# Layer 1 on one Trainium2 core: chosen rows moved by rank with indirect DMAs instead of products with a selection matrix, and GpSimd's products in pairs

## The chip, the core and the metric

The kernel runs on one core of a Trainium2 chip. A core has a matrix engine (PE in the profile, its weight loads PEld), a vector engine (DVE), a scalar engine (ACT), a general engine (POOL, GpSimd) and a queue engine that issues most transfers (SP). Each runs its own instruction list in order; they meet through semaphores, and sixteen DMA engines move data between the device's memory and SBUF. The time is the device time of the whole program in microseconds; lower is better.

## The reference, cut to what matters

The input is (8, 512, 256) in float32. Layer 0 (gated linear attention and a mixture of experts) is untouched by the change. Layer 1 adds two branches to its input: a selective state-space scan, and a mix of light local attention over windows of 128 rows and heavy attention of 256 chosen rows of each batch element against all 512:

```
xn = _layernorm(x)
x  = x + L1_attn(xn) + L1_ffn(xn)

# L1_attn: state-space scan, 512 channels x 16 states, over 512 steps
h = exp(delta[..., None] * A) * h + delta[..., None] * B[:, None, :] * u[..., None]
y = einsum('bds,bs->bd', h, C)
out = einsum('btm,dm->btd', (y + D*u) * silu(z), W_out)

# L1_ffn
light_out = light_local_attn(x, ...)
scores_q, idx_q = route(x, q_routing_token, NQ)      # NQ = 256 of the 512 rows
routed_q = take_along_axis(x, idx_q)
routed_out = heavy_attn(routed_q, x, ...)
heavy_out = zeros_like(x).at[arange(b)[:, None], idx_q].set(routed_out)
return light_out + heavy_out
```

Each row's *rank* by its score decides whether it is chosen (rank under 256) and in which place it stands among the chosen.

## The kernel before, in words

Layer 0 takes the first 770 us or so; then layer 1 runs one batch element after the other, with the stages of neighbouring elements overlapping. Every engine's list in layer 1 is written from one table, `AT` (`FIRST` and `LAST` for the first and last element): it gives each step of an element a number, the steps of all elements (number plus `PERIOD` times the element) are sorted, and every engine issues its own steps in that sorted order. The numbers set an order only. PSUM banks 3 to 7 are dealt out in the same order (`Banks`); banks 0 to 2 belong to the scan.

**The scan.** The 512x16 states are cut into 64 chunks of 128 partitions by 512 steps. For chunk n, POOL writes the drive (`dbu`, `drive`, L2042) into slot n mod 8 of the ring `HB`; ACT writes the decay (`dA`) into a PSUM bank; DVE scans (`scan`, L2596). The product with C is DVE's for even chunks (`mult`, L2601) and POOL's for odd ones (`cg`, `times_c`, L2048). PE sums four chunks at a time over the states (`fold`), which frees four slots of the ring: a drive waits for the fold of two groups before. Then come `skip` (DVE), `gate` (POOL, L2052), and `tail` (PE), the output product. POOL also does `del` and `du` (L2068, L2075) for the next element.

**The attention.** Projections, scores, maxima, exponentials, transposes (`turn`), values, normalisation and the output product (`widen`) run for four light tiles and two heavy ones. The light results are added to `X` by DVE (`widenc`), the heavy ones go to `YR` (`widenr`, ACT).

**The chosen rows.** DVE counts the rank of each row (`rank`, `ranks`: L2579 to L2590). POOL turns the ranks into a 0/1 matrix `Sel` of 4x128 rows by 256 places (`sel`, L2062). PE multiplies the rows with it (`xg`, `gather`: eight products of 128x256), which gives the chosen rows already transposed. PE also transposes `Sel` (`st`, L2172, eight transposes), ACT copies it to `SelT` (`sta`, `stv`), and in `tail` two products with `SelT` per tile of 128 rows add the heavy outputs back at their rows in the same PSUM bank. `tailc` (DVE) adds the bank to `X`, `out` stores it, and `x_ld` loads the next element's `X` once all four tiles are stored. Float32 products run as two instructions each in the trace, so eight products appear as x16; transposes appear once.

Layer 0 already has indirect DMAs of this kind: POOL scatters rows of 1 KB to device memory by a slot number (`sca`, L581) and gathers them back while adding (`gad`, L591).

## Time and profile before

| | us |
|---|---|
| median of 3 runs | 1994.58 (1978.45 to 1995.64) |
| the profiled execution, its own time | 2009.35 |
| its span | 2007.2 |
| PE busy | 1817.3 (91%) |
| DVE busy | 1566.5 (78%) |
| POOL busy | 1504.5 (75%) |
| ACT busy | 1345.0 (67%) |

The shares are averages over two layers with different limits. From about 930 us to 1820 us the trace of layer 1 repeats with a period of 148.5 us; that stretch is where an average of one period can be read. Matmuls are pipelined and their ends are modelled, so a busy PE is not PE at its peak.

### The profile page before, as it was taken

How to read it: one execution, taken by the hardware profiler on the slowest of the kernel's cores; microseconds unless marked ns; L12 is line 12 of the kernel's file. 1: busy time of each engine (PE TensorE's matmuls, PEld its weight loads, DVE VectorE, ACT ScalarE, POOL GpSimd, SP SyncE). 2: the span in 40 equal slices, each digit the busy share in tenths (PEclk: the TensorE clock that was granted, in tenths of full speed). 3: DMA queues.
4: the chain of work that ended last, by engine and by line, in shares of the span. 5: the costliest groups of instructions: out<-in, count | busy, mean ns of one | idle time of the engine just before them, and what ended most of it. 6: DMA issues, size and time to landing. Idle time of an engine off the chain costs nothing.

```text
span 2007.2 us, 44199 instructions
## 1 busy us (share of the span) xinstructions
PE 1817.3 (91%) x13543; PEld 1159.6 (58%) x13543; DVE 1566.5 (78%) x2833; ACT 1345.0 (67%) x3152; POOL 1504.5 (75%) x1211
## 2 busy tenths in 40 slices
PE   6889989989999947897999999999999999998897
PEld 4577777767777724543644644644644644644554
DVE  5766756666666543899899889999999989988896
ACT  3465456337546426687788788788888788787674
POOL 2834663593557431789989989989989989988996
PEclk9888889679888878898999999999999999999899
DMA  8234244344525575333642732642633644542530
GB/s 276 86 99 125 73 115 138 73 111 112 127 61 140 131 179 166 97 101 112 178 127 90 179 113 90 174 117 98 172 112 109 160 118 120 144 133 96 143 84 22
DMA packets 162135, 245.76 MB, mean 122 GB/s; under 512 B 32712, under 2 KB 107112, under 8 KB 161904
## 3 DMA queue, kind: packets, MB, share of 16 engines
q1 hardware_dynamic: 149616, 226.15, 39.7%
q0 software_dynamic: 12288, 16.79, 4.2%
q8 instruction: 113, 1.85, 0.4%
q14 instruction: 118, 0.97, 0.2%
HBM read 169.39 MB, written 73.47 MB: 121 GB/s over the span
## 4 chain that ended last, share of the span: by engine, by line
PE 28%; POOL 13%; issue 8%; DVE 6%; DMA 4%; ACT 2%; SPq 2%; POOLq 0%; DVEq 0%; ACTq 0%
PE bank L2097 24%; POOL HB L2042 8%; POOL HB L2048 4%; PE bank L2200 2%; DVE bank L2596 2%; SPq L1973 2%; DVE HB L2596 1%; DMA BC<-ssm_scratch 1%; DMA X<-x_scratch 1%; POOL SD L2068 1%; DMA out<-X 1%; PE bank L2106 1%; DMA dd_scratch<-U 1%; POOL U L2075 1%; PE bank L2228 1%
## 5 line engine op out<-in xcount | busy, mean ns | idle before, releaser
L2042 POOL TENSOR_TENSOR HB<-DD,BC 128x512 f32<-128x512 f32 x512 | 642.8, 1281 | 81.0 <-PE bank L2097 60.4
L2388 ACT ACTIVATE bank<-DD,A 128x512 f32<-128x512 f32 x512 | 351.9, 691 | 114.7 <-DVE HB L2601 61.5
L2048 POOL TENSOR_TENSOR HB<-HB,BC 128x512 f32<-128x512 f32 x256 | 324.5, 1281 | 20.3 <-DVE HB L2596 20.3
L2596 DVE TENSOR_TENSOR_SCAN bank<-bank,HB 128x512 f32<-128x512 f32 x256 | 311.4, 1216 | 32.8 <-ACT bank L2388 18.9
L2596 DVE TENSOR_TENSOR_SCAN HB<-bank,HB 128x512 f32<-128x512 f32 x256 | 310.4, 1212 | 19.9 <-POOL HB L2042 15.8
L2601 DVE TENSOR_TENSOR HB<-bank,BC 128x512 f32<-128x512 f32 x256 | 175.7, 686 | 15.3 <-DVE bank L2596 0.5
L2097 PE MATMUL bank<-HB,fold 128*32 128x512 f32 x1024 | 140.9, 622 | 33.8 <-POOL HB L2048 17.7
L591 POOL DMA_INDIRECT X<-expert_out_scratch,slot x64 | 101.2, 1580 | 54.5 <-DMA expert_out_scratch<-YS 39.1
L2200 PEld LDWEIGHTS bank<-ident,PR 128*128 128x128 f32 x768 | 89.3, 144 | 76.3 <-issue 44.1
L2097 PE MATMUL bank<-Ka,Qa 64*128 64x128 f32 (+1 forms) x768 | 112.9, 413 | 16.0 <-ACT PT L2322 14.2
L2200 PE MATMUL bank<-ident,PR 128*128 128x128 f32 x768 | 115.8, 283 | 12.3 <-ACT PR L2426 10.3
L557 POOL TENSOR_TENSOR ROW<-ROW,COL 128x1024 f32<-128x1024 f32 x32 | 66.6, 2082 | 80.0 <-DMA ROW<-row_scratch 67.4
L2097 PE MATMUL bank<-Wv,XRT 128*128 128x512 f32 x256 | 124.8, 621 | 0.1
L2097 PE MATMUL bank<-XRT,Wk 128*128 128x512 f32 x256 | 123.0, 606 | 1.1 <-ACT Qa L2402 0.7
L2097 PE MATMUL bank<-XT,edge 128*128 128x512 f32 x256 | 121.0, 611 | 3.3 <-ACT SD L2322 2.2
L2322 ACT ACTIVATE PT<-bank 128x512 f32<-128x512 f32 x192 | 109.4, 591 | 8.2 <-PE bank L2200 6.6
L2097 PEld LDWEIGHTS bank<-PT,Va 128*64 128x64 f32 x1536 | 83.0, 137 | 47.6 <-issue 37.0
L620 PE MATMUL bank<-v,AT 64*64 64x16 f32 x2048 | 93.8, 237 | 16.1 <-DVE S L1230 6.9
L571 POOL TENSOR_SCALAR XSC<-edge,weight 128x256 f32<-128x256 f32 x64 | 62.0, 977 | 57.0 <-DVE weight L1178 55.8
L620 PEld LDWEIGHTS bank<-v,AT 64*64 64x64 f32 x2048 | 89.2, 180 | 25.6 <-issue 20.8
L2097 PE MATMUL bank<-PT,Va 128*64 128x128 f32 x1536 | 102.4, 279 | 0.1
L2426 ACT ACTIVATE PR<-bank,nmax 128x512 f32<-128x512 f32 x128 | 87.0, 682 | 20.2 <-DVE nmax L2620 20.1
(280 smaller groups left out, 4218.4 us busy)
## 6 DMA issues: line engine op xcount, KB each, us to landing
DD<-dd_scratch SPq DMA_DIRECT2D x512, 128.0 KB, 3.6
ROW<-row_scratch SPq DMA_DIRECT2D x64, 256.0 KB
BC<-ssm_scratch SPq DMA_DIRECT2D x128, 128.0 KB, 4.9
US<-us_scratch SPq DMA_DIRECT2D x32, 512.0 KB, 5.5
XL<-sorted_scratch SPq DMA_DIRECT2D x92, 128.0 KB, 2.7
expert_out_scratch<-YS SPq DMA_DIRECT2D x92, 128.0 KB, 1.9
us_scratch<-U SPq DMA_DIRECT2D x8, 1024.0 KB, 4.2
us_scratch<-SD SPq DMA_DIRECT2D x8, 1024.0 KB, 6.5
```

The source lines that it names most:

```text
L557: done(pool.tensor_tensor(ROW[:, t % 2], ROW[:, t % 2], bc(COL[:, t], CH), ALU.subtract), "df")
L591: pool.indirect_dma_start(X[:, b % 2, t], None, scr["expert_out"][g % 2], bass.IndirectOffsetOnAxis(slot[:, g % 2, x, c:c + 1], 0), comput ...
L620: return pe.matmul(out, lhsT, rhs, start=start, stop=stop)
L2042: done(pool.tensor_tensor(HB[:, c % HR], du, bc, ALU.mult), "dbu")
L2048: done(pool.tensor_tensor(h, h, bc, ALU.mult), "cg")
L2097: return pe.matmul(out, lhsT, rhs, start=start, stop=stop)
L2200: q = pe.transpose(bank[:, j * P:(j + 1) * P], PR[:, m % 2, j * P:(j + 1) * P], ident[:])
L2322: done(act.activation(dst, banks.of[made, b, i][:], ACT.Copy), copy)
L2388: done(act.activation(PD[n % 2][:], delta, ACT.Exp, scale=A[:, k:k + 1]), "dA")
L2426: done(act.activation(PR[:, m % 2], banks.of["score", b, m][:], ACT.Exp, bias=nmax[:, m % 4, 0:1], accum_out=sums[:, a, h:h + 1]), "exp")
L2596: done(dve.tensor_tensor_scan(h if n % 2 else dA, dA, h, 0.0, ALU.mult, ALU.add), "scan")
L2601: done(dve.tensor_tensor(HB[:, (NCH * b + n) % HR], PD[n % 2][:], bc, ALU.mult), "mult")
```

## The change

1. **Pairs on POOL.** `dbu` now writes two chunks with one instruction of 128x1024 (32 per element instead of 64), and `cg` multiplies two odd chunks at once (slots c and c+2; 16 instead of 32). A scan waits for the pair, a `cg` for both of its scans.
2. **Choosing.** `Sel`, `SelT`, `sel`, `st`, `sta`, `stv` are gone. DVE copies the ranks to integers (`slot`). POOL scatters the four tiles of rows by rank to device memory (`scat`, four indirect DMAs), SP loads the first 256 places as `XQ` (`ql`), and PE transposes them (four transposes instead of eight products).
3. **Adding.** SP stores `YR` to device memory (`ys`), whose places 256 to 511 were zeroed once at the start, and POOL gathers all 512 rows by rank and adds them to `X` (`gad`, four indirect DMAs). `tail` is left with the products of the scan; `tailc` waits for the gather of its tile.
4. The table of numbers is another one.

Its core:

```diff
-PERIOD = 177.597
+PERIOD = 212.24
 AT = {
...
+    "slot": [-12.224],
+    "scat": [-6.013, -11.242, -0.19, -11.573],
+    "gad": [236.605, 243.002, 261.958, 243.453],
+    "ql": [26.232],
+    "ys": [234.633],
...
                 def h_load(b):
-                    after(sp, "xg", b - 1, 0)
+                    after(sp, "xrt", b - 1, *range(ND))
+                    sp.wait_ge(moved["rows_out"], 16 * NT * b)
...
+                def chosen_load(b):
+                    sp.wait_ge(moved["rows_out"], 16 * NT * (b + 1))
+                    after(sp, "xg", b - 1, 0)
+                    sp.dma_start(XQ[:], scr["ranked"][b % 2][0:NQ].rearrange("(j p) d -> p j d", p=P)).then_inc(over["q_in"], 16)
+
+                def chosen_store(b):
...
+                    after(sp, "widenr", b, *range(NQT))
...
+                    sp.dma_start(scr["heavy_out"][b % 2][0:NQ].rearrange("(j p) d -> p j d", p=P), YR[:]).then_inc(over["y_out"], 16)
...
-                def drive(b, n):
+                def drive(b, i):
...
-                    done(pool.tensor_tensor(HB[:, c % HR], du, bc, ALU.mult), "dbu")
+                    du = DD[:, g % DDS:g % DDS + 2, 1]
+                    done(pool.tensor_tensor(HB[:, c % HR:c % HR + 2], du, bc.unsqueeze(1).broadcast_to([P, 2, T]), ALU.mult), "dbu")
...
-                    after(pool, "scan", b, n)
-                    done(pool.tensor_tensor(h, h, bc, ALU.mult), "cg")
+                    h = HB[:, c:c + 3:2]
+                    after(pool, "scan", b, n, n + 2)
+                    done(pool.tensor_tensor(h, h, bc.unsqueeze(1).broadcast_to([P, 2, T]), ALU.mult), "cg")
...
-                def select(b, t):
...
-                    done(pool.tensor_scalar(Sel[:, t], numbers[:], ties[:, t:t + 1], None, ALU.is_equal), "sel")
+                def rank_rows(b, t):
+                    after(pool, "slot", b, 0)
+                    after(pool, "xr", b, t)
...
+                    pool.indirect_dma_start(scr["ranked"][b % 2], bass.IndirectOffsetOnAxis(slot[:, b % 2, t:t + 1], 0),
+                                            XN[:, t], None).then_inc(moved["rows_out"], 16)
+
+                def add_heavy_rows(b, t):
+                    after(pool, "widenc", b, t)
+                    pool.wait_ge(over["y_zero"], 32)
+                    pool.wait_ge(over["y_out"], 16 * (b + 1))
+                    pool.indirect_dma_start(X[:, t], None, scr["heavy_out"][b % 2],
+                                            bass.IndirectOffsetOnAxis(slot[:, b % 2, t:t + 1], 0),
+                                            compute_op=ALU.add).then_inc(moved[f"heavy_add{t}"], 16)
...
-                        for t in range(NT):
-                            q = mm(bank[:, k * NQ:(k + 1) * NQ], XN[:, t, k * P:(k + 1) * P], Sel[:, t],
-                                   t == 0, t == NT - 1)
+                        for j in range(NQT):
+                            q = pe.transpose(bank[:, k * NQ + j * P:k * NQ + (j + 1) * P], XQ[:, j, k * P:(k + 1) * P], ident[:])
...
-                    for j in range(NQT):
-                        q = mm(bank[:, 0:D], SelT[:, j, t * P:(t + 1) * P], YR[:, j], False, j == NQT - 1)
...
+                def slots(b):
+                    after(dve, "ranks", b, 0)
...
+                    done(dve.tensor_copy(slot[:, b % 2], ties[:]), "slot")
...
                 def tail(b, t):
                     after(dve, "tail", b, t)
-                    after(dve, "widenc", b, t)
+                    dve.wait_ge(moved[f"heavy_add{t}"], 16 * (b + 1))
```

The order of instructions at three places. In these rows HB<-DD,BC is a drive, HB<-HB,BC a product with C, "Wout,G" the tail's products of the scan, "YR,SelT" those of the heavy outputs.

First, POOL where one element ends and the next begins. Before:

```order
L2042 TENSOR_TENSOR HB<-DD,BC 128x512
L2048 TENSOR_TENSOR HB<-HB,BC 128x512 x2
L2062 TENSOR_SCALAR Sel<-numbers,ties 128x256
L2048 TENSOR_TENSOR HB<-HB,BC 128x512 x2
L2042 TENSOR_TENSOR HB<-DD,BC 128x512 x5
L2048 TENSOR_TENSOR HB<-HB,BC 128x512 x2
L2042 TENSOR_TENSOR HB<-DD,BC 128x512
L2052 TENSOR_TENSOR G<-G,US 128x512
L2042 TENSOR_TENSOR HB<-DD,BC 128x512 x4
L2048 TENSOR_TENSOR HB<-HB,BC 128x512 x2
L2042 TENSOR_TENSOR HB<-DD,BC 128x512 x2
L2062 TENSOR_SCALAR Sel<-numbers,ties 128x256
```

After:

```order
L2079 DMA ranked_scratch<-edge,slot 512x256
L2056 TENSOR_TENSOR HB<-DD,BC 128x1024 x2
L2064 TENSOR_TENSOR HB<-HB,BC 128x2x512
L2056 TENSOR_TENSOR HB<-DD,BC 128x1024
L2068 TENSOR_TENSOR G<-G,US 128x512
L2056 TENSOR_TENSOR HB<-DD,BC 128x1024 x2
L2086 DMA X<-heavy_out_scratch,slot 128x256
L2064 TENSOR_TENSOR HB<-HB,BC 128x2x512
L2086 DMA X<-heavy_out_scratch,slot 128x256 x2
L2056 TENSOR_TENSOR HB<-DD,BC 128x1024 x2
L2064 TENSOR_TENSOR HB<-HB,BC 128x2x512
L2086 DMA X<-heavy_out_scratch,slot 128x256
```

Each drive or product in the second list covers two chunks. Three more scatters stand just ahead of the second list; the gathers that add stand among the first drives of the next element, as one, two and one.

Second, PE at the tails and the choice of rows. Before:

```order
L2097 MATMUL bank<-Wout,G 128x256 x4
L2097 MATMUL bank<-YR,SelT 128x256 x2
L2097 MATMUL bank<-HB,fold 32x512 x4
L2200 MATMUL bank<-ident,PR 128x128 x4
L2097 MATMUL bank<-Wout,G 128x256 x4
L2097 MATMUL bank<-YR,SelT 128x256 x2
L2228 MATMUL bank<-ident,RX 128x128 x4
L2200 MATMUL bank<-ident,PR 128x128 x4
L2097 MATMUL bank<-Ka,Qa 128x128 x8
L2172 MATMUL bank<-ident,Sel 128x128 x4
L2097 MATMUL bank<-Sel,edge 128x256 x8
L2097 MATMUL bank<-HB,fold 32x512 x4
```

After:

```order
L2219 MATMUL bank<-ident,PR 128x128 x8
L2125 MATMUL bank<-Ka,Qa 128x128 x8
L2125 MATMUL bank<-Wout,G 128x256 x4
L2125 MATMUL bank<-HB,fold 32x512 x4
L2191 MATMUL bank<-ident,XQ 128x128 x4
L2125 MATMUL bank<-Wout,G 128x256 x8
L2125 MATMUL bank<-PT,Va 64x128 x8
L2219 MATMUL bank<-ident,PR 128x128 x4
L2148 MATMUL bank<-ident,edge 128x128 x4
L2219 MATMUL bank<-ident,PR 128x128 x4
```

The products with SelT and Sel and the transposes of Sel are gone, and four transposes of XQ stand between the tails.

Third, the end of POOL's list. Before:

```order
L2042 TENSOR_TENSOR HB<-DD,BC 128x512 x4
L2048 TENSOR_TENSOR HB<-HB,BC 128x512
L2042 TENSOR_TENSOR HB<-DD,BC 128x512
L2048 TENSOR_TENSOR HB<-HB,BC 128x512 x3
L2052 TENSOR_TENSOR G<-G,US 128x512
```

After:

```order
L2056 TENSOR_TENSOR HB<-DD,BC 128x1024 x2
L2064 TENSOR_TENSOR HB<-HB,BC 128x2x512
L2056 TENSOR_TENSOR HB<-DD,BC 128x1024
L2064 TENSOR_TENSOR HB<-HB,BC 128x2x512
L2086 DMA X<-heavy_out_scratch,slot 128x256
L2068 TENSOR_TENSOR G<-G,US 128x512
L2086 DMA X<-heavy_out_scratch,slot 128x256 x3
```

A gather now stands ahead of the last gate, and three behind it.

## Rows read from the trace of the kernel before

**Rows 1.** Busy time by engine in two periods of layer 1: PE, PEld, DVE, ACT, POOL (instructions).
```profile
1229.50:1378.00 148.50, 142.05 (x812) 79.25 (x808) 134.54 (x182) 122.26 (x265) 137.76 (x110) 1.00 0.46 129
1378.00:1526.50 148.50, 142.44 (x814) 79.26 (x811) 137.22 (x182) 123.42 (x266) 138.21 (x110) 1.00 0.46 129
```

**Rows 2.** Chain that ended last: start, us, what; over one period of layer 1.
```profile
1230.07 2.34 POOL SD L2068
...
1274.46 9.03 PE bank L2097 x44
...
1323.58 19.41 PE bank L2097 x80
...
1378.61 2.34 POOL SD L2068
```

**Rows 3.** PE groups by shape, 1274 to 1304 us alone: busy, mean ns | idle before, releaser.
```profile
L2097 PE MATMUL bank<-YR,SelT 128*128 128x256 f32 x16 | 4.1, 379 | 0.0
...
L2097 PE MATMUL bank<-Sel,edge 128*128 128x256 f32 x16 | 3.6, 379 | 0.0
...
L2172 PE MATMUL bank<-ident,Sel 128*128 128x128 f32 x8 | 1.3, 279 | 0.0
```

**Rows 4.** POOL groups by shape, one period, 1229.5 to 1378 us.
```profile
L2042 POOL TENSOR_TENSOR HB<-DD,BC 128x512 f32<-128x512 f32 x65 | 81.6, 1279 | 9.6 <-PE bank L2097 7.4 <-DMA DD<-dd_scratch 2.2
...
L2048 POOL TENSOR_TENSOR HB<-HB,BC 128x512 f32<-128x512 f32 x32 | 40.5, 1280 | 0.9 <-DVE HB L2596 0.9
...
L2062 POOL TENSOR_SCALAR Sel<-numbers,ties 128x256 f32<-128x256 f32 x4 | 3.7, 929 | 0.0
...
L2075 POOL TENSOR_TENSOR U<-SD,U 128x1024 f32<-128x1024 f32 x2 | 4.7, 2360 | 0.2
```

**Rows 5.** POOL groups by shape, whole span: layer 0's indirect DMAs and a 1024-wide operation.
```profile
L591 POOL DMA_INDIRECT X<-expert_out_scratch,slot x64 | 101.2, 1580 | 54.5 <-DMA expert_out_scratch<-YS 39.1 <-issue 13.3 <-DMA X<-expert_out_scratch,slot 0.9
...
L581 POOL DMA_INDIRECT sorted_scratch<-XSC,slot x64 | 67.0, 1046 | 14.6 <-issue 8.6 <-POOL XSC L571 5.7 <-DVE edge L1054 0.3
...
L557 POOL TENSOR_TENSOR ROW<-ROW,COL 128x1024 f32<-128x1024 f32 x32 | 66.6, 2082 | 80.0 <-DMA ROW<-row_scratch 67.4 <-DVE COL L1082 12.4
```

**Rows 6.** L561 on POOL: duration ns min/median/max, first and last start.
```profile
L561 POOL TENSOR_TENSOR ROW<-ROW,later x32: 2333/2400/2947, 38.6 to 650.5; 128x1024 f32<-128x1024 f32 x32
```

**Rows 7.** DMA issues of the whole span: KB each, median us to landing.
```profile
out<-X SPq DMA_DIRECT2D x32, 128.0 KB, 1.9
...
X<-expert_out_scratch,slot POOLq DMA_INDIRECT x64, 3.9
```

**Rows 8.** DVE in the ranking: durations ns min/median/max, then L2583 as a group.
```profile
L2583 DVE SCALAR_TENSOR_TENSOR Sel<-KR,KC,before x32: 346/528/5334, 837.9 to 1854.9; 128x128 f32<-128x128 f32 x32
...
L2590 DVE TENSOR_TENSOR ties<-ties,ahead x8: 164/1146/1151, 842.5 to 1857.9; 128x4 f32<-128x4 f32 x8
...
L2583 DVE SCALAR_TENSOR_TENSOR Sel<-KR,KC,before 128x128 f32<-128x128 f32 x32 | 29.4, 920 | 0.0
```

**Rows 9.** Timeline around 1242 us, DVE then POOL: start, duration.
```profile
1241.34 1.10 DVE L2583 SCALAR_TENSOR_TENSOR Sel<-KR,KC,before 128x128 f32<-128x128 f32 x1
...
1239.78 2.51 POOL L2048 TENSOR_TENSOR HB<-HB,BC 128x512 f32<-128x512 f32 x2
```

**Rows 10.** Waits, 1229.5 to 1378 us: us in total, times, longest.
```profile
DVE bank L2596 <- POOL HB L2042: 3.0, 3, 2.0
...
DVE HB L2596 <- POOL HB L2042: 2.1, 4, 1.1
```

**Rows 11.** Timeline of the end, POOL then PE.
```profile
1992.48 1.27 POOL L2052 TENSOR_TENSOR G<-G,US 128x512 f32<-128x512 f32 x1 [2.51 <-DVE G L2609]
...
1991.52 1.99 PE L2097 MATMUL bank<-Wao,OT 128*128 128x256 f32 x8
...
1994.03 1.97 PE L2097 MATMUL bank<-Wout,G 128*128 128x256 f32 x8 [0.52 <-POOL G L2052]
...
2003.61 1.03 PE L2097 MATMUL bank<-YR,SelT 128*128 128x256 f32 x4
```

610 lines of the change are left out of this document (307 added, 303 removed), and 162 rows, old and new, of tables (AT, FIRST, LAST).

## The prediction, made before the changed kernel was timed

> **What bounds the kernel now.** I read the busy time in 10-us and 148.5-us stretches first, then the chain of waits, then the groups by shape inside one period, then the waits.
>
> Layer 0 is not touched, so everything is decided after 770 us. There the trace repeats: the same step of POOL stands in the chain at 1230.07 and at 1378.61 us [rows 2], so one batch element costs 148.5 us. In that period PE is busy for 142.0 to 142.4 us, POOL for 137.8 to 138.2, DVE for 134.5 to 137.2, ACT for about 123 [rows 1]; the clock of PE is at its full level (1.00, the 2.4 GHz one), so there is nothing to gain or lose there. Four engines are within 19 us of each other: the reader should expect that taking work from one shows up only until the next one is reached. The chain inside the period runs over PE from 1274.46 us on (stretches of 9.0 us, later 19.4 us [rows 2]) up to 1343 us, and over POOL's drives in most of the rest. I read it as: PE sets the pace for half of a period, POOL for a third.
>
> **What the change does to PE.** Removed per element: the products with SelT (4.1 us busy), the products with Sel (3.6), the transposes of Sel (1.3) [rows 3]. Added: four transposes of XQ, half of those 1.3 us, 0.65. Net -8.4 us, and all of them stand between 1274 and 1304 us [rows 3], inside the stretch where the chain is on PE. PE goes from 142.2 to 133.8 us. ACT loses two copies, about 1.2 us, and is not near the bound.
>
> **POOL.** A drive and a product with C take 1.28 us each [rows 4]; 96 of them make 122.9 us. The change makes 48 of 1024 columns. Nothing in the trace has their form exactly. Nearest is the plain 128x1024 product in the same stretch, 2.36 us [rows 4]; the one that reads an operand again and again, as the pair reads BC, has a median of 2.40 [rows 6]. The ends: 2.08 us (an operand that stands still for 64 columns [rows 5]) and 2.56 us (two singles, nothing saved). I take 2.40: 115.2 us, so -7.7 (ends -23.1 and 0). The four `sel` go: -3.7 [rows 4]. Four scatters at 1.05 and four adding gathers at 1.58 us [rows 5] come: +10.5. Before such a DMA POOL also stood idle for reasons other than the transfer it waited for: (14.6 + 54.5 - 39.1) us over 128 of them [rows 5], 0.23 each, +1.9. Sum: +1.0, so POOL goes from 138.0 to 139.0 us. POOL is not relieved at all; the pairs only pay for the DMAs. With the ends of the pair's price it is 123.6 to 146.7.
>
> **DVE.** Its removed and added work is one tiny copy (`slot`). But rows show a coupling: an operation of the ranking that reads two SBUF tensors takes 0.35 us at its shortest and 0.92 in the mean, and the tiny addition after it 1.15 instead of 0.16 [rows 8]. The one of 1.10 us ended at 1242.44, where POOL's instruction ended at 1242.29 [rows 9]: it waited for the end of what POOL was doing. Per element that is 4 x 0.57 + 1.0 = 3.3 us. When most of POOL's instructions are twice as long, a wait for the end of one is twice as long in the mean: +3.3, and `slot` may meet it too, +1. Bounds: 0 and, if every such operation met a whole pair, 6 x 2.4 = 14 less the 3.3 there now. DVE goes from 135.9 to 140.2 us. (The Trainium skill, SBUF — State Buffer, section "Who interferes with whom", has the rule behind it: GpSimd and a VectorE instruction with two SBUF inputs lock a shared port pair for the whole instruction, and the later one blocks. The trace agrees in rows 9. By a rule of shared bandwidth instead, DVE would gain no time at all and the 4.3 us would be absent from the sum.)
>
> **The new waits.** I followed each through the orders.
> - Choosing: ranks, `slot`, scatter, load, transposes. Scatters stand at the end of POOL's element, the load and the transposes after several drives of the next one. Landings of this kind take 2 to 4 us [rows 7]; covered by the drives between them (some five pairs, 12 us).
> - Adding: `ys` needs the last `widenr`, the gathers need `ys` landed, `tailc` needs the gather landed (3.9 us [rows 7]). Behind each gather stand one or two pairs or gathers on POOL before the scan that follows `tailc` on DVE can start anyway, so DVE should lose nothing. Behind a waiting gather on POOL stand the drives; the first fold of the element lies between `widen` and the gather, which covers the store.
> - `x_ld` waits for all four stores and now comes later in the element; SP has the slack (its next load of DD is needed some ten drives later). Until `widenc` the first light banks stay taken; that is the least certain cover.
> - Scans wait for a pair instead of a single drive: the first of a pair 1.1 us later, the second 0.2 earlier. A product with C waits for both scans, so the fold and the four slots of the ring come about 1.1 us later, of a turn of the ring of 18.5 us (148.5/8).
>
> **The period.** DVE is now the fullest with 140.2 us. It waited 5.1 us for POOL's drives in a period [rows 10]; POOL in turn waited 7.4 us for folds [rows 4], which come sooner on a lighter PE, while the pairs work the other way. I take 4.6 of waits: 144.8 us, -3.7 per element, -29.6 over eight.
>
> **The end.** Now the last gate runs at 1992.48, the tails start at 1994.03 and follow each other by 2.6 us [rows 11]. The tails shrink by 1 us each, three of them count: -3. The output product before them starts at 1991.52 and would come some 2 us sooner, but a gather now stands ahead of the last gate and needs the copy of that product, its store (2 to 3 us, [rows 7] with twice the size) and its own 1.58 us, so the gate comes 4 to 5 us later than without: +1.5 in all. At the start two stores of zeros go beside other work: 0.
>
> Sum -28. The profiled execution took 2009.35 us, 14.8 over the median of the three runs; the same difference applied to the median gives 1994.6 - 28 = **1966 us**, chance 0.42, its own range 1950 to 1980.
>
> **Rivals.**
> - *PE's time passes through.* If DVE's 12.6 idle us are slack and its operations slip into POOL's gaps, the period falls by PE's 8.4 us to 140.1: 1994.6 - 67 + 1.5 = 1929 us (1915 to 1950). For it: the chain hardly touches DVE. Against: POOL at 139.0 would need a share of 99%. Chance 0.19.
> - *The gain is used up.* DVE's 140.2 us keep 8.3 of their 12.6 us of waits and the period stays 148.5: about 1995 us (1975 to 2014). For it: every engine's order is new, and banks are held longer. Chance 0.20.
> - *POOL becomes the bound (slower).* If a pair costs what two singles do, 2.56 us, POOL has 146.7 us; with its waits for DD and scans (3.1) 149.8, with those for folds (7.4) 157. The middle, 153.4: +4.9 x 8 + 1.5 = 2035 us. It decides from a price of about 2.53 us a pair (139.0 - 115.2 + 48p + 3.1 = 148.5). Against it: the 1024-wide product in this very stretch takes 2.36. Chance 0.15.
> - *The DMAs on POOL wait for DVE (slower).* If writing a transfer's description waited for one scan of 1.2 us each time, eight of them make 9.8 us and POOL has 148.8, with 3.1 of waits 151.9: +3.4 x 8 + 1.5 = 2023 us. Against it: in layer 0, beside a DVE busy for 65%, a gather needed 1.58 us in the mean of 64 [rows 5]. Chance 0.04. (The Trainium skill, SBUF — State Buffer, section "SBUF: two separate sides", warns of it for VectorE's two-port modes; no row here shows it.)
>
> **The numbers.** About 1% is what a measurement of this kernel tells from no change, 20 us. Faster (under 1974.6): 0.35 of the forecast's 0.42 and the 0.19 of the first rival, 0.54. Within: 0.07 and 0.20, 0.27. Slower: 0.19. The range 1925 to 2015 leaves out the low end of the first rival (about 0.05) and the two slower ones mostly (0.15).
>
> **What the new profile would show.** PE about 134 us per period, with no SelT. Pairs on POOL of 2.36 to 2.40 us; at 2.5 and over, the POOL rival. Scatters and gathers at 1.05 and 1.6 us; longer, the last one. L2583's successor with a mean near 1.5 us. The distance of two `slot` copies is the period: 140, 145 or 148.5 tells the cases apart. If `tailc` waits for a gather, if POOL waits for the store of YR outside the last element, or if `widenc` waits over a microsecond for X, my reading of the orders was wrong. A period under 139 or over 157 would overthrow the whole account.

## The result, and the profile after

The changed kernel takes **2032.98 us** (median of 3, 2029.21 to 2035.48), against 1994.58: ratio 1.0177, 95% interval 1.0118 to 1.0236. The forecast was 1966 with a range up to 2015; it is slower, and outside the range.

The profiled execution took 2029.21 us. Layer 0 ends at another time in each execution (732 and 713 us), so I compare layer 1 alone: 1274.8 us before, 1314.9 after, +40.1. Up to the last gate of the first element it is 8.7 us more, over the six periods behind it 23.2, over the rest (one more period and the end) 8.2: the loss is in every element. The end alone, from the input of the very last gate on, got shorter, 15.5 to 14.4 us.

Busy time over three periods, before and then after (columns as in [rows 1]):

```profile
1119.13:1565.20 446.07, 426.27 (x2420) 237.60 (x2419) 406.02 (x543) 367.48 (x792) 411.97 (x327) 1.00 0.45 128
```

```profile
1117.81:1577.32 459.51, 414.62 (x2313) 221.61 (x2313) 421.43 (x547) 362.15 (x786) 413.01 (x196) 0.99 0.48 135
```

Per element PE went down by 3.9 us only (142.1 to 138.2, at a clock that is no longer full all the time), DVE up by 5.1 (135.3 to 140.5), POOL stayed (137.3 to 137.7). The period went up by 4.5. **DVE's idle time did not shrink**: (446.07 - 406.02)/3 = 13.4 us before, (459.51 - 421.43)/3 = 12.7 after. POOL's grew from 11.4 to 15.5.

The groups of POOL in that stretch, where [rows 4, 5] had the forecast's prices:

```profile
L2056 POOL TENSOR_TENSOR HB<-DD,BC 128x1024 f32<-128x1024 f32 x96 | 230.4, 2441 | 9.7 <-PE bank L2125 9.4
L2064 POOL TENSOR_TENSOR HB<-HB,BC 128x1024 f32<-128x1024 f32 x49 | 121.1, 2471 | 31.2 <-DVE HB L2605 31.2
L2086 POOL DMA_INDIRECT X<-heavy_out_scratch,slot x12 | 19.0, 1581 | 2.4 <-issue 1.9 <-DVE HB L2605 0.5
...
L2079 POOL DMA_INDIRECT ranked_scratch<-edge,slot x12 | 12.2, 1020 | 2.9 <-issue 1.7 <-DVE slot L2599 1.0 <-PE bank L2125 0.2
```

A pair lasts 2.36 us where no DMA stands before it; behind a DMA the record is some 0.6 us longer, because it begins before the DMA's record ends. So the means of 2.44 and 2.47 hold part of the DMAs. What is new is the wait of the products with C for scans: 31.2 us in three elements, 10.4 each, against 1.7 before (0.9 in the one period of [rows 4]). The waits of the drives for folds fell from 8.3 to 3.1. The sum of the two rose.

DVE in the ranking, where [rows 8] stood:

```profile
L2584 DVE SCALAR_TENSOR_TENSOR KJ<-KR,KC,before 128x128 f32<-128x128 f32 x12 | 22.4, 1863 | 0.0
L2599 DVE CAST slot<-ties 128x4 int32<-128x4 f32 x3 | 4.5, 1493 | 0.0
L2590 DVE TENSOR_TENSOR ties<-ties,ahead 128x4 f32<-128x4 f32 x3 | 3.5, 1177 | 0.0
```

And the timeline (start, duration) around the longest of them, first DVE, then POOL:

```profile
1231.40 5.86 DVE L2584 SCALAR_TENSOR_TENSOR KJ<-KR,KC,before 128x128 f32<-128x128 f32 x1
```

```profile
1230.11 4.70 POOL L2101 TENSOR_TENSOR U<-SD,U 128x1024 f32<-128x1024 f32 x2
1234.76 2.35 POOL L2056 TENSOR_TENSOR HB<-DD,BC 128x1024 f32<-128x1024 f32 x1
1240.81 2.35 POOL L2064 TENSOR_TENSOR HB<-HB,BC 128x1024 f32<-128x1024 f32 x1 [3.70 <-DVE HB L2605]
```

An operation that takes 0.34 us alone took 5.86. It did not end with the POOL instruction that ran when it started (until about 1232.5), nor with the next one (1234.8), but at 1237.26, after the third, behind which POOL first had a gap (1237.11). Then POOL stood idle for 3.70 us, waiting for a scan that stood behind this very operation in DVE's list.

A gap is not what it needs, though. Two elements later the same operation started beside the same instructions of POOL, again without a gap between them, and ended behind the first of them:

```profile
1540.93 1.23 DVE L2584 SCALAR_TENSOR_TENSOR KJ<-KR,KC,before 128x128 f32<-128x128 f32 x1
```

```profile
1539.63 4.74 POOL L2101 TENSOR_TENSOR U<-SD,U 128x1024 f32<-128x1024 f32 x2
1544.33 2.42 POOL L2056 TENSOR_TENSOR HB<-DD,BC 128x1024 f32<-128x1024 f32 x1
```

So it is let in at the end of a POOL instruction, but not at every one. No run here shows what decides it.

**Stages.** To see where a period gets longer I cut it at every eighth of its 64 scans on DVE (starts in the timeline, mean of four periods in the middle of layer 1; stage 1 begins with the first scan after the last gate's input). "Old order" and "new order" are the two tables of numbers; the kernels are told with the experiments.

| kernel | ratio to before | 1 | 2 | 3 | 4 | 5 | 6 | 7 | 8 | period |
|---|---|---|---|---|---|---|---|---|---|---|
| before | 1 | 14.3 | 16.7 | 21.1 | 20.5 | 15.5 | 20.7 | 23.4 | 16.3 | 148.4 |
| after | 1.018 | **19.3** | 16.9 | 19.7 | 18.8 | 15.5 | 19.4 | **26.3** | 17.0 | 152.9 |
| pairs, old order | 1.023 | 14.5 | 18.0 | 21.6 | 19.5 | 16.6 | 20.5 | 25.1 | 16.3 | 152.0 |
| DMAs, old order | 1.036 | **21.6** | 16.8 | 20.8 | 20.4 | 15.5 | 20.7 | 24.5 | 16.3 | 156.6 |
| both, old order | 1.050 | **21.4** | 17.7 | 21.5 | 19.4 | 16.6 | 20.5 | 25.3 | 16.4 | 158.7 |
| DMAs, new order | 1.035 | 19.0 | 18.6 | 20.5 | 18.8 | 15.4 | 21.0 | 27.9 | 17.7 | 158.9 |
| drives in pairs only | 1.014 | 14.7 | 17.0 | 20.5 | 19.8 | 17.7 | 19.4 | 26.3 | 15.7 | 151.3 |
| products in pairs only | 1.005 | 14.2 | 16.4 | 21.8 | 19.9 | 14.5 | 21.6 | 23.9 | 16.5 | 148.8 |
| less PE, stages 1 to 2 | 0.998 | 14.5 | 17.8 | 20.8 | 20.8 | 15.5 | 20.7 | 23.4 | 16.1 | 149.5 |
| less PE, stages 3 to 4 | 0.990 | 14.4 | 16.1 | 20.2 | **19.3** | 15.5 | 20.7 | 23.4 | 16.5 | 146.0 |
| more POOL, stage 1 | 1.018 | **18.8** | 15.9 | 20.3 | 20.8 | 15.5 | 20.7 | 23.4 | 16.3 | 151.7 |
| more POOL, where idle | 1.003 | 14.3 | 16.6 | 20.0 | 20.9 | 15.5 | 20.7 | 23.4 | 16.4 | 147.7 |
| late gathers, old order | 1.018 | **14.4** | 16.2 | 20.8 | 21.8 | 15.5 | 20.7 | 24.5 | 16.2 | 150.1 |
| after, no gathers | 1.007 | 16.5 | 16.1 | 19.8 | 18.8 | 15.3 | 20.0 | 26.2 | 16.6 | 149.3 |
| after, no scatters | 1.017 | 19.4 | 17.5 | 19.6 | 18.8 | 15.3 | 19.6 | 25.3 | 16.8 | 152.2 |
| after, no DMAs | 1.004 | 16.6 | 16.1 | 19.8 | 18.8 | 15.4 | 19.5 | 27.5 | 15.6 | 149.2 |
| the same, one input | 0.991 | 16.5 | 16.1 | 19.8 | 18.8 | 15.8 | 19.6 | **23.1** | 15.5 | 145.0 |
| late gathers, new order | 1.018 | 16.5 | 16.1 | 19.8 | 18.8 | 17.2 | 19.0 | 27.3 | 16.7 | 151.3 |
| ranking moved | 1.024 | 19.3 | 17.5 | 19.7 | 18.8 | 15.4 | 19.6 | 27.5 | 17.0 | 154.6 |
| all three | 1.021 | 16.5 | 16.1 | 19.8 | 20.2 | 16.9 | 19.0 | 24.8 | 18.8 | 152.1 |

The period is one of the profiled execution; the ratio comes from timed runs beside the kernel before on the same chip, and holds layer 0 too. Stage 1, where the gathers stand, and stage 7, where the ranking stands, lose 5.0 and 2.9 us; stages 3, 4 and 6 win 4.4. Periods of one execution differ among themselves by up to 5 us (146.9 to 151.9 before), so a microsecond between two rows says little.

The 26.3 us of stage 7 are a mean of two cases. Over the four elements the first ranking operation took 5.86, 5.85, 1.23 and 1.22 us, stage 7 lasted 28.0, 29.2, 24.0 and 24.0, and the period 154.0, 155.7, 149.8 and 152.1. Stage 7 with the long wait and without it (columns as in [rows 1]):

```profile
1382.22:1411.45 29.23, 23.70 (x111) 11.39 (x110) 28.99 (x42) 14.68 (x31) 21.41 (x11) 0.88 0.44 135
1537.22:1561.25 24.03, 19.56 (x107) 9.33 (x106) 23.79 (x42) 14.57 (x31) 21.40 (x11) 1.00 0.52 164
```

DVE is busy for all but a quarter of a microsecond of it both times, so what the ranking waits there lengthens the period. The long wait comes in every row of the new order that keeps this operation, in one to four of the four elements, and in none of the old order (2.3 us at most; outside these four, the ranking of the last element in the kernel before has one, of 5.33 us [rows 8]). Pairs are not needed for it: with single products in the new order it came in all four, 6.1 to 7.8 us long:

```profile
1223.95 7.75 DVE L2586 SCALAR_TENSOR_TENSOR KJ<-KR,KC,before 128x128 f32<-128x128 f32 x1
```

### The profile page after: what moved, and what is told of

Same layout as the page of the kernel before. It is cut to its first block, busy times and chain, and to the rows that moved or that the text cites. A ratio compares the mean times of both kernels' runs of the same rounds, so it can differ in the third digit from the quotient of the medians.

```text
span 2027.5 us, 43158 instructions
## 1 busy us (share of the span) xinstructions
PE 1777.8 (88%) x13255; PEld 1111.7 (55%) x13255; DVE 1603.1 (79%) x2840; ACT 1333.1 (66%) x3136; POOL 1504.4 (74%) x859
## 4 chain that ended last, share of the span: by engine, by line
PE 18%; DVE 16%; POOL 13%; issue 11%; ACT 4%; DMA 1%; POOLq 0%; DVEq 0%; SPq 0%; ACTq 0%
PE bank L2125 15%; POOL HB L2056 6%; POOL HB L2064 5%; DVE bank L2605 4%; DVE HB L2605 3%; DVE KJ L2584 2%; PE bank L2219 2%; DVE U L2567 1%; POOL X L2086 1%; DVE nmax L2629 1%; DVE HB L2610 1%; POOL G L2068 1%; PE bank L2134 1%; ACT bank L2399 1%; DVE ties L2590 1%
## 5 line engine op out<-in xcount | busy, mean ns | idle before, releaser
L2056 POOL TENSOR_TENSOR HB<-DD,BC 128x1024 f32<-128x1024 f32 x256 | 610.3, 2422 | 61.2 <-PE bank L2125 43.1
L2064 POOL TENSOR_TENSOR HB<-HB,BC 128x1024 f32<-128x1024 f32 x128 | 312.7, 2443 | 69.8 <-DVE HB L2605 69.8
L2610 DVE TENSOR_TENSOR HB<-bank,BC 128x512 f32<-128x512 f32 x256 | 175.8, 687 | 15.8 <-issue 0.2
L2219 PE MATMUL bank<-ident,PR 128*128 128x128 f32 x768 | 121.9, 292 | 55.3 <-ACT PR L2437 34.9
L2125 PE MATMUL bank<-Ka,Qa 64*128 64x128 f32 (+1 forms) x768 | 117.2, 427 | 19.0 <-ACT SSM L2376 9.1
L2125 PE MATMUL bank<-Wao,OT 128*128 128x256 f32 x384 | 97.4, 398 | 8.7 <-DVE OT L2645 8.7
L2430 ACT ACTIVATE PR<-bank,nmax 128x128 f32<-128x128 f32 x256 | 91.0, 367 | 19.0 <-DVE nmax L2626 18.8
```

The source lines that it names most:

```text
L2056: done(pool.tensor_tensor(HB[:, c % HR:c % HR + 2], du, bc.unsqueeze(1).broadcast_to([P, 2, T]), ALU.mult), "dbu")
L2064: done(pool.tensor_tensor(h, h, bc.unsqueeze(1).broadcast_to([P, 2, T]), ALU.mult), "cg")
L2125: return pe.matmul(out, lhsT, rhs, start=start, stop=stop)
L2219: q = pe.transpose(bank[:, j * P:(j + 1) * P], PR[:, m % 2, j * P:(j + 1) * P], ident[:])
L2430: done(act.activation(PR[:, m % 2, cols], banks.of["score", b, m][:, cols], ACT.Exp, bias=nmax[:, m % 4, j:j + 1], accum_out=sums[:, m // ...
L2610: done(dve.tensor_tensor(HB[:, (NCH * b + n) % HR], PD[n % 2][:], bc, ALU.mult), "mult")
```

## The experiments

The letters name theories, each told where it is first expected. Ratios are to the kernel before, which was timed again beside each run.

**Which part costs.** Four kernels take the change apart. "Old order" is the table of before, with the pairs and DMAs put in at the place of what they replace.

```diff
# pairs_old_order: before, with the pairs alone
-    done(pool.tensor_tensor(HB[:, c % HR], du, bc, ALU.mult), "dbu")
+    done(pool.tensor_tensor(HB[:, c % HR:c % HR + 2], du, bc.unsqueeze(1).broadcast_to([P, 2, T]), ALU.mult), "dbu")
# dma_old_order: after, products single, AT/FIRST/LAST of before, and in them
+    slot=[-20.229], scat=[-18.448, -8.981, -5.0, -14.006], gad=[196.0, 190.5, 191.5, 193.2], ql=[8.0], ys=[187.5]
# both_old_order: both;  dma_new_order: after with every pair split in two
```

> The kernel before with only its drives and products with C in pairs, each pair at the place of its earlier drive or its later product in the old order; choosing and adding stay products. Theory W (pairs make new waits: a product with C now waits for both scans, in the changed kernel POOL waits 69.8 us for scans instead of 20.3, and DVE operations with two SBUF inputs wait for longer POOL instructions, 55.0 us instead of 29.4): slower than the kernel before by 3 to 6 us per element, 25 to 50 us. Theory O (the new order of all engines is what costs): within 10 us of the kernel before, or faster by the 7 us per element that POOL saves. Theory D (the indirect DMAs on POOL cost): the same as O here, faster.

> The changed kernel with single drives and products, in the old order; scatters stand where the selection was made, gathers ahead of the last steps of the tail. Theory W: PE's 8.4 us per element are released without new waits, 10 to 50 us faster than the kernel before, though POOL now carries 12.4 - 3.7 = 8.7 us more per element (138 to 147 us in 148.5). Theory D: slower by 20 to 60 us, since POOL becomes the bound near 147 us plus 3 to 10 us of waits. Theory O: faster or the same, like W.

> The whole change (pairs and DMAs) in the old order. Theory O: faster than the kernel before by 10 to 40 us, so at least 50 us faster than the changed kernel. Theory W or D: within 15 us of the changed kernel, 2015 to 2045 us.

> The changed kernel with its own order, but every pair split into two single instructions that stand next to each other. Theory W: the waits for pairs and the longer holding of DVE go, faster than the changed kernel by 15 to 40 us, though POOL pays 7.7 us per element more. Theory D: slower than the changed kernel, POOL at 147 us plus waits, 2040 to 2090 us. Theory O: the same as the changed kernel within 15 us.

Measured, as ratios with intervals: pairs alone 1.0231 (1.0185 to 1.0276), DMAs alone 1.0362 (1.0304 to 1.0419), both 1.0505 (1.0462 to 1.0549), DMAs in the new order with single products 1.0354 (1.031 to 1.0397). So in the old order each half of the change costs by itself, and the two nearly add up (1.059 by the sum). The new order is no cost there: with both in place it wins back 3.3 points of the 5.0. With single products it wins nothing (1.0354 against 1.0362), so in the new order the pairs are a gain: 1.0177 with them. Of the theories W was right for the pairs alone and failed for the DMAs; D had the direction of both runs with the DMAs and single products, with more than its 20 to 60 us in the old order (some 70); O failed; and none had both in the old order, some 98 us slower than the kernel before. In the run with the DMAs alone PE had its relief and POOL 7.4 us more, and the period grew by 8.2: the relief bought nothing. The table shows 7.3 of it in stage 1, 14.3 to 21.6. What DVE's scans waited there was the drives; three elements each, before and then with the DMAs (us in total, times, longest):

```profile
DVE HB L2596 <- POOL HB L2042: 5.9, 11, 1.1
```

```profile
DVE HB L2622 <- POOL HB L2075: 32.1, 21, 3.8
```

**Which pairs cost.** Old order, one kind in pairs each.

```diff
# drive_pairs_only
-    after(dve, "dbu", b, n)
+    after(dve, "dbu", b, n // 2)
# product_pairs_only
-    after(pool, "scan", b, n)
+    after(pool, "scan", b, n, n + 2)
```

> The kernel before, in its own order, with the drives alone in pairs of 128x1024; the products with C stay single. Theory P (POOL sets the pace: an element's period is POOL's busy time plus its waits, 137.3 + 11.4 us before): 16 pairs per element that would have 2.36 us each for two drives of 1.282 save 16 x 0.2 = 3.2 us of POOL per element, and a pair's first drive does not wait for a scan, so waits grow by at most 1 to 2 us: period 146 to 147, the whole 10 to 20 us below the kernel before. Theory E (the prediction's: PE folds and the chain through them set the pace, POOL is off it): no change, within 5 us. Theory W (any pair delays the first of two scans by half of its 2.4 us, so the pair costs wherever it stands): DVE's wait for HB of the drives grows by some 5 us per element, the whole 20 to 45 us slower, as with all products in pairs (ratio 1.0231).

> The kernel before, in its own order, with the products with C alone in pairs. Theory P: 8 x 2 x 0.2 = 3.2 us of POOL per element saved, but a pair must wait for the second of two scans, which took 8.4 us per element of waits with all in pairs against 1.7 before: waits grow by 5 to 8 us, period 150.5 to 153.5, the whole 20 to 40 us slower. This and the run with the drives alone in pairs would then add up to the run with both (+46 us). Theory E: no change within 5 us. Theory W: slower by 10 us or less, since the scans themselves are not delayed by these pairs.

Measured 1.0138 (1.0066 to 1.0211) and 1.0046 (1.0007 to 1.0085). My theory P failed on both: in the first POOL was busy for 4.1 us less per element, and the period grew by 2.8; the second cost under 1%, not 20 to 40 us. POOL as the pacer of the whole period is as wrong as PE was. Theory W had both sizes, but only a part of the mechanism for the drives. The wait of scans for them did rise, from 3.7 to 6.0 us per element, yet the time is lost in stages 5 (2.2) and 7 (2.9). In stage 7 no scan waits for a drive. DVE is busy there for 2.9 us more, before and then with the drives in pairs:

```profile
1379.76:1403.05 23.29, 22.31 (x119) 11.62 (x118) 22.55 (x44) 16.66 (x34) 23.13 (x17) 1.00 0.39 135
```

```profile
1372.75:1398.92 26.17, 22.84 (x120) 11.57 (x118) 25.44 (x43) 16.47 (x34) 25.64 (x16) 1.00 0.38 129
```

These are the four ranking operations: 3.5 us per element together before, 6.3 with the drives in pairs, 5.2 with all in pairs, 4.0 with the products' alone, while stage 7 rose by 2.9, 1.7 and 0.5. In stage 5 scans wait 0.7 us longer for drives and 1.7 for ACT's decays.

**Is PE the pacer?** Nearly the same time of PE left out in two places, all else kept. In less_pe the chosen rows and the heavy outputs' addition are left out, in less_in_proj half of each in-projection's sum.

```diff
# less_pe (stages 1 and 2)
-    for t in range(NT):
-        q = mm(bank[:, k * NQ:(k + 1) * NQ], XN[:, t, k * P:(k + 1) * P], Sel[:, t], t == 0, t == NT - 1)
+    for t in range(NQT):
+        q = pe.transpose(bank[:, k * NQ + t * P:k * NQ + (t + 1) * P], XN[:, t, k * P:(k + 1) * P], ident[:])
...
-    q = mm(bank[:, 0:D], SelT[:, j, t * P:(t + 1) * P], YR[:, j], False, j == NQT - 1)
# less_in_proj (stages 3 and 4)
-    for m in range(ND):
+    for m in range(1):
```

> The kernel before, with work of PE left out and nothing added: the heavy experts' outputs are not added in the tail (no products with SelT), and the first 256 rows are taken by transposes in the place of the chosen rows by products with Sel. POOL and DVE keep every instruction. PE has some 7 us less per element. Theory P (POOL sets the pace): no change, within 10 us. Theory E (PE sets the pace for half of a period, the prediction's reading of the chain): the period falls by about the 7 us, the whole 50 to 60 us faster.

> The kernel before with only the first of the two products summed in each in-projection (XT,edge: 16 of 32 products per element left out, 16 x 0.46 = 7.4 us of PE per element), all else kept. These stand in the stage in which PE is at 1.00 busy and POOL at 0.56, whereas the 7 us that the run with less of PE left out stood in the first stages, where POOL is at 1.00. Theory S (each stage has its own pacer): now a part of it is gained, 3 to 6 us per element, the whole 25 to 50 us below the kernel before. Theory N (PE sets the pace nowhere): no change within 8 us, as with less_pe (0.998).

Measured 0.998 (0.9933 to 1.0028) and 0.9898 (0.9859 to 0.9937). In stages 1 and 2 PE's time is worth nothing that can be measured: theory E, the prediction's own, failed. In the other place it is worth something, though a third of it: 7.4 us removed, 2.4 gained, mostly in stages 2 to 4, a little under what theory S gave. There 6.1 of the 7.4 us left PE's busy time, at a clock of 1.00. In less_pe less arrives, because PE gets a lower clock. Two rows of less_pe, then the stretch of the kernel before that answers to the second:

```profile
1118.81:1566.77 447.96, 413.31 (x2342) 225.02 (x2341) 404.57 (x545) 366.87 (x793) 412.70 (x328) 0.98 0.46 128
1131.20:1156.00 24.80, 20.69 (x134) 13.79 (x133) 21.00 (x27) 18.62 (x47) 21.40 (x18) 0.86 0.62 170
```

```profile
1131.50:1156.20 24.70, 22.35 (x145) 15.41 (x143) 21.13 (x27) 19.10 (x50) 21.62 (x18) 0.93 0.61 172
```

Of some 7 us of products only 4.3 left the busy time (426.27 to 413.31 in three elements), and the mean granted clock of these 25 us (stages 1 and 2) fell from 0.93 to 0.86. In less_pe the clock went to the lower level, 1.2 GHz, behind five microseconds in which PE was busy for 1.65:

```profile
1135.00:1140.00 5.00, 1.65 (x20) 1.25 (x16) 4.06 (x7) 3.92 (x8) 5.00 (x5) 1.00 0.36 101
1140.00:1147.00 7.00, 6.27 (x30) 3.39 (x31) 5.48 (x7) 4.61 (x19) 5.95 (x6) 0.51 0.72 196
```

**Does POOL's work cost by its place?** The kernel before with five more instructions on POOL per element that nobody reads, at two places of the order.

```diff
+    elif what == "more":
+        done(pool.tensor_tensor(spare[:, i], kinv[:, 0:NT], half[:], ALU.pow), "more")
# more_early: AT["more"] = [12.9, 13.9, 15.6, 17.0, 18.4]; more_idle: AT["more"] = [74.0, 74.6, 75.2, 75.8, 76.4]
```

> The kernel before with five more small instructions on POOL per element (128x4 to a spare tensor that nobody reads, the form that takes 1.05 us a piece where the norms use it, 5.2 us per element), among the first drives of the period, where POOL is 100% busy in the kernel before and where the indirect adds of the other runs stand. Theory S (POOL sets the pace stage by stage: its work costs in full where its drives are what the scans wait for, nothing where it waits for a fold): the first eight scans of the period take 5 us longer (14.4 before), the others as long as before; the whole 8 x 5.2 = 42 us, 35 to 45 us slower. Theory M (POOL's work is bounded by the mean of the period, 11.4 us of idle time per element): under 10 us slower.

> The same five instructions per element, put where POOL waits for a fold in the kernel before (5.4 us, once per element, before the drives of chunk 32). Theory S: hidden in that wait, within 8 us of the kernel before. Theory M: the same as with them among the first drives. Theory B (any work of POOL costs in full, wherever it stands): 42 us slower, as there.

Measured **1.0177** (1.0132 to 1.0223) and **1.0033** (0.9997 to 1.0068). These are the plainest two runs of the study: the same work, 4.9 us per element, costs 35 us of the whole in stage 1, and in the wait 8, with no cost at all inside the interval. Stage 1 went from 14.3 to 18.8 in the first and stayed at 14.3 in the second, as theory S had it. The wait, in the kernel before and with the work in it (timeline of POOL):

```profile
1329.08 2.51 POOL L2042 TENSOR_TENSOR HB<-DD,BC 128x512 f32<-128x512 f32 x2 [5.37 <-PE bank L2097]
```

```profile
1300.40 4.93 POOL L2092 TENSOR_TENSOR spare<-kinv,half 128x4 f32<-128x4 f32 x5
1305.72 2.52 POOL L2046 TENSOR_TENSOR HB<-DD,BC 128x512 f32<-128x512 f32 x2 [0.40 <-PE bank L2103]
```

Stage 1 of one element, in before, after, with the DMAs in the old order, and with the gathers moved away (next experiment but one):

```profile
1272.27:1286.48 14.21, 13.58 (x79) 10.17 (x77) 13.97 (x19) 10.92 (x29) 14.21 (x13) 1.00 0.36 89
```

```profile
1272.46:1291.73 19.27, 17.42 (x110) 10.82 (x106) 14.80 (x21) 17.02 (x53) 18.64 (x11) 1.00 0.52 128
```

```profile
1265.69:1287.30 21.61, 13.12 (x76) 8.82 (x74) 14.30 (x20) 10.92 (x29) 20.97 (x17) 0.84 0.48 106
```

```profile
1261.06:1275.46 14.40, 11.63 (x65) 8.05 (x62) 14.00 (x20) 10.91 (x29) 14.40 (x12) 0.88 0.37 97
```

In before, POOL is busy for all of the 14.21 us (fifth number with an x). With the DMAs in the old order the same eight scans take 14.30 us of DVE and 20.97 of POOL: POOL alone sets this stage. In the changed kernel POOL is busy for 18.64 us of 19.27.

**Gathers or scatters?** The changed kernel without one kind, or both. Without the gathers the heavy outputs are not added; without the scatters the first 256 rows are loaded.

```diff
# no_gathers
-    elif what == "gad":
-        add_heavy_rows(b, i)
# no_scatters
-    elif what == "scat":
-        rank_rows(b, i)
-    sp.dma_start(XQ[:], scr["ranked"][b % 2][0:NQ].rearrange("(j p) d -> p j d", p=P))
+    sp.dma_start(XQ[:], scr["xn2"][b][0:NQ].rearrange("(j p) d -> p j d", p=P))
```

> The changed kernel without its eight indirect DMAs per element: the first 256 rows are loaded in the place of the chosen ones, and the heavy experts' outputs are not added. Ranks and slots are still computed, pairs and order stay. POOL has 4 x 1.02 + 4 x 1.58 = 10.4 us less per element and the 1.9 us of gaps beside them. Theory P: period 153.9 - 12 = 142 (bounded by DVE's 140.5 busy, so rather 143 to 147), the whole 55 to 95 us below the changed kernel. Theory O (the new order and the pairs' waits are what costs, the DMAs on POOL lie in its waits): at most 20 us below the changed kernel, still slower than the kernel before.

> The changed kernel without its four indirect adds per element: the heavy experts' outputs are not added. POOL has 4 x 1.58 = 6.3 us less per element and the gaps beside them, all in the first stage of the period (eight scans, 19.3 us in the changed kernel, 14.4 in the one before). Without any of the eight DMAs it was 2010.96 us. Theory S: nearly all that these eight cost comes from the adds, since the scatters stand where POOL waits for scans anyway: 2010 to 2020 us. Theory D (each DMA costs by its time on POOL): 6.3 of 10.4 parts of the 22 us, about 2020 us, and the rest with the scatters.

> The changed kernel without its four scatters per element: the first 256 rows are loaded in the place of the chosen ones. The counterpart of the run without the adds. Theory S: within 8 us of the changed kernel (2025 to 2035 us). Theory D: 4.1 of 10.4 parts of the 22 us, about 2024 us, and equal to the run without the adds within their intervals.

Measured: without all eight 1.0041 (1.0004 to 1.0078), without gathers 1.0065 (1.0036 to 1.0093), without scatters 1.0174 (1.0128 to 1.022), beside 1.0177 with all. The gathers cost 1.1 points, some 22 us; the scatters, at 4 x 1.0 us of POOL, nothing that can be seen, as theory S had it. I had expected 12 us per element from all eight (theory P); 3.7 came (152.9 to 149.2), some 27 us of the whole, more than theory O's 20. POOL then waited 11.4 us for folds and 11.5 for scans. Stage 7 hides a part of the gain: the long ranking wait came in three of the four elements there, and in two of the changed kernel's (28.7 us with it, 24.0 without; the one period without it took 146.3).

**Are they costly where POOL waits?** X gets two buffers, the tail adds to X first, the gathers follow later. With that the load of X also waits for older stores only, and the rows go out later; the two runs don't tell these apart from the place of the gathers. In stage 1 the difference can be read from POOL's busy time, which went from 20.97 to 14.40 us in the old order.

```diff
-    after(pool, "widenc", b, t)
+    after(pool, "tailc" if b < B - 1 else "widenc", b, t)
-    pool.indirect_dma_start(X[:, t], None, scr["heavy_out"][b % 2], ...
+    pool.indirect_dma_start(X[:, b % 2, t], None, scr["heavy_out"][b % 2], ...
# late_gathers_old: gad = [251.7, 252.5, 253.3, 259.0]; late_gathers_new: gad = [307.6, 308.2, 308.8, 327.2]
```

> All products single, the old order, the eight indirect DMAs, as in the run dma_old_order (1.0362 of the kernel before), but the four indirect adds stand some 50 us later, where POOL waits for a fold (5.4 us): X has two buffers, the tail adds to X first, the heavy outputs are added after it, and the rows go out behind that (the last element keeps its order). Theory S: the first stage goes back from 21.6 to 14.4 us and 6.3 us of adds fit into the wait but for 1 to 2 us: period 149 to 151, ratio 1.00 to 1.015. Theory B (the adds cost by their time on POOL or by their traffic, wherever they stand): the ratio stays at 1.03 to 1.04.

> The changed kernel, pairs and new order, with the same move of the four indirect adds: three of them where POOL waits 4.55 us for a scan before the seventh product with C, one before the ninth. Theory S: close to the run without the adds (1.0065 of the kernel before): 1.005 to 1.012. Theory B: stays at 1.015 to 1.02, the changed kernel's. At 1.005 it would be faster than the changed kernel and still not than the one before.

Old order: 1.0177 (1.0093 to 1.0261) against 1.0362 where they stood before, half of the loss gone; stage 1 is back to 14.40, the period 150.1 as expected, though the ratio is over the 1.015 that I gave. The gathers last as long as ever (1576 ns); POOL's waits for folds went from 9.1 to 2.7 us per element. New order: 1.0175 (1.0091 to 1.0259), no gain that the measurement can tell, as theory B had it and not theory S, although the profiled period fell from 152.9 to 151.3. Stage 1 gave back 2.7 us. Stage 5 took 1.7, with 1.6 of waiting for ACT's decays in it; the 1.0 of stage 7 is the long ranking wait in three of four elements instead of two.

**Is the ranking on the path?** The kernel without the eight DMAs, with the operation that reads two SBUF tensors replaced by one with a single input (ties within a tile are not counted). Then the changed kernel itself with the ranking moved behind two scans, and at last with all the repairs together.

```diff
# no_dmas_one_input
-    own(dve.scalar_tensor_tensor(out=KJ[:, 1, 0:P], in0=KR[:, own_tile], scalar=KC[:, t:t + 1], in1=before[:], ...
+    own(dve.tensor_scalar(KJ[:, 1, 0:P], KR[:, own_tile], KC[:, t:t + 1], None, ALU.not_equal, ALU.min, ...
# rank_moved, all_three
+AT["rank"] = [-20.5, -21.341, -26.177, -26.25]
# all_three, too: the last addition writes the slots
+    done(dve.tensor_tensor(slot[:, b % 2], ties[:], ahead[:, 0], ALU.add), "ranks")
```

> The changed kernel without its eight indirect DMAs (the first 256 rows are loaded, the heavy outputs aren't added), and the ranking's operation with two SBUF inputs (2.12 us mean, 4 per element, beside POOL's products in pairs) replaced by one with one input, so that ties within a tile are not counted. Theory L (the wait of that operation for POOL's pairs is on the path): DVE 4 x 1.8 = 7 us per element less, the period from 149.9 to 143 to 147, the whole 25 to 55 us below the 2010.96 us with it. Theory S: DVE's ranking stands in the last stage, where DVE has 6 to 10% of slack; 0 to 15 us below.

> The changed kernel with one edit in the table of the order: DVE's four ranking steps stand after the two scans that follow them in the changed kernel, and so behind POOL's run of four instructions of 2.37 us, beside which the first ranking operation took 5.86 us for what takes 0.34 us alone. Theory L: that operation falls to about 1 us, 3 to 5 us of DVE per element less, half of it on the path (as in the run without that operation): 12 to 20 us below the changed kernel, 1.008 to 1.012 of the kernel before. Theory K (another POOL instruction takes the place: POOL has hardly a gap there, and the operations wait as long as before): within 8 us of the changed kernel, the ranking operation's mean still over 1.5 us.

> The changed kernel with the ranking moved as in the other run, the cast to the slots made by the last addition of the ranks (1.49 us of DVE per element less), and the four indirect adds together where POOL waits for a scan before the seventh product with C (X in two buffers). If the causes add up: stage one back to 16.5 us, 27 us for the ranking's and 10 to 20 us for the adds' part: 1.000 to 1.008 of the kernel before, faster than the changed kernel by 1 to 1.7%. If they don't (each freed stage hands its time to the next engine that is full): 1.01 to 1.02.

Measured: 0.9907 (0.987 to 0.9944) against 1.0041 (each beside the kernel before on its own chip), 27 us for one kind of operation; stage 7 fell from 27.5 to 23.1. It is on the path. But moving it did not help, 1.0241 (1.0199 to 1.0283): theory K held in its mechanism, with some 13 us over the changed kernel by the ratios, where it allowed 8 (the intervals overlap). The wait went along in three of the four elements, now 6.37 us, up to the end of a third POOL instruction again (1241.41, POOL's at 1241.27):

```profile
1235.04 6.37 DVE L2587 SCALAR_TENSOR_TENSOR KJ<-KR,KC,before 128x128 f32<-128x128 f32 x1
```

All three repairs give 1.021 (1.0167 to 1.0252). Stage 1 is short (16.5) and DVE has 3 us less to do, but the ranking operation still has a mean of 1671 ns and stages 4, 5 and 8 took 4.6 us. The causes do not add up. No version that computes everything beat the kernel before; the two that are clearly ahead of it leave work out.

## Why the prediction was wrong

- **The step that failed** is "PE sets the pace for half of a period", and with it "I take 4.6 of waits" in place of 12.6. PE's relief lay between 1274 and 1304 us, that is in stages 1 and 2. There the chain ran through PE, but in stage 1 POOL was busy for 14.21 of 14.21 us and DVE for 13.97: three engines were full at once, and a chain shows only one of them. Removing 7 us of products from PE there gives nothing (0.998). DVE's idle time per period went from 13.4 to 12.7 us where the sum had it fall to 4.6, so its added 5.1 us came on top: the period grew by 4.5 us instead of falling by 3.7.
- **Sums over a period.** I weighed POOL's -11.4 against its +12.4 and got +1.0. The sum was right (137.7 measured, 139.0 forecast) and useless: the pairs save everywhere, also where POOL waits, and the gathers stand in stage 1, where in the old order all of their 6.3 us and the gaps beside them count (+7.3); in the new one leaving them out shortens it by 2.8. The two runs with five extra instructions show that it is the place.
- **"Scans wait for a pair": under-sized.** I put 1.1 us on the first scan of a pair and nothing on the period. The wait of scans for drives rose by 2.3 us per element with drives in pairs alone, in the old order. That run cost 1.4%, but of the 5.1 us that its stages 5 and 7 lose 2.9 are the ranking's wait in stage 7.
- **DVE +4.3** was right in size (140.5 us, forecast 140.2); L2584's mean came to 1.72 us in the whole span (forecast 1.5). The mechanism was only half right. I had a wait for the end of one POOL instruction, twice as long when these are. The four operations took 1.6 us per element more by the pairs in the old order (forecast 2.3); the rest came from waits over two or three POOL instructions, which all kernels in the new order have, that with single products too. The bound of "a whole pair" each (2.4 us) was passed at 5.86. In the sum the term was to be paid out of waits that shrink; but it stands in stage 7, where DVE has no waits to give (22.55 us busy of 23.29 before). Taking the operation out gave some 27 us.
- **Prices of single instructions** all held: pair 2.36 to 2.37 us (2.40), gathers 1.58 (1.58), scatters 1.02 (1.05).
- **Covers** held in the steady part: `tailc` never waited for a gather there, POOL never for the store of YR. The one wait for a gather that mattered is at the end (DVE, then PE's tails); PE's first tails, from 2015.22 on, cover a part of it.

```profile
2021.26 0.75 DVE L2655 TENSOR_TENSOR X<-X,bank 128x256 f32<-128x256 f32 x2 [7.43 <-DMA X<-heavy_out_scratch,slot]
```

```profile
2015.22 9.68 PE L2125 MATMUL bank<-Wout,G 128*128 128x256 f32 x32 [2.21 <-POOL G L2068]
```

- **The end**, +1.5 in the sum, was -1.1 from the last gate's input on. The gather ahead of the last gate (1.60 us, from 2011.95) did not hold the gate up: its input came later, and it began at 2013.91 after 0.35 us of waiting for it.
- **PE's term.** Of the 8.4 us forecast 3.9 arrived, the clock being 0.99 over the periods and down to 0.84 in stage 1 of the run with the DMAs in the old order. "Nothing to gain or lose there" was wrong: where this PE was relieved in stages 1 and 2, it lost clock.
- **The rivals.** None of the four is what happened. The forecast of POOL as the bound came near in time (2035) by luck: it needed pairs of 2.53 us, and they took 2.36. "The gain is used up" had DVE's waits staying in part, 8.3 us of them, and is the nearest in mechanism; 12.7 stayed.

Still open: what decides at which POOL instruction's end the ranking operation is let in, and why the new order brings the long wait; why scans wait for ACT's decays in stage 5 with drives in pairs; the 2.2 us of stage 1 that remain in the new order without the gathers (1.6 of waiting for an ACT decay, in the late-gathers run); and why moving the gathers in the new order gave nothing in the timed runs. The new order was not run with the old way of choosing and adding.

## What to carry to other kernels

Where four engines are busy for over 80% of a period, cut the period into stages before pricing a change, and ask for each edit which engine is at 100% in its stage: the sum over a period tells little. A chain of waits names one engine where several are full; before believing that it sets the pace, look at the others' busy time in the same 15 us. Work added to an engine should go into its longest wait (here 5.4 us for a fold), and the cheapest experiment for that is a few dummy instructions put at both places. It is a first try and no promise: it halved the loss in the old order and gained nothing measurable in the new one. Before reading a mean over periods, look whether it mixes two cases, as stage 7 did.
